# State-space stage of a two-layer kernel: gate copy, score taking and residual adding placed one or two states later, and eight constant products ahead of the first row of C

## The reference, cut to what matters

```python
xz = x @ W_in.T;  xs, z = split(xz)
xc = silu(causal_conv4(xs) + conv_b)
dt, Bm, Cm = split(xc @ W_x.T, [64, 80])
dt = softplus(dt @ W_dt.T + b_dt);  A = -exp(A_log)
h[l, d, n] = exp(dt[l, d] * A[d, n]) * h[l-1, d, n] + dt[l, d] * Bm[l, n] * xc[l, d]
y = sum_n h[l, d, n] * Cm[l, n] + D_param * xc
x = x + ga * ((y * silu(z)) @ W_out.T)
```

## Time and profile before

| | us |
|---|---|
| median of 3 runs | 663.12 (655.6 to 663.97) |
| the profiled execution: its device time | 653.8 |
| the profiled execution: its span in the profile | 651.7 |
| ahead of the state-space loop on VectorE | 32 |
| state-space loop on VectorE | 32 to 278 |
| experts of layer 0, from the first transposed rows to the last row written | 302 to about 403 |
| layer 1 up to its experts, and they | about 403 to 651 |

### The profile page before, as it was taken

How to read it: one execution, slowest core, us unless ns; L and a number is a source line. 1 busy time by engine, 2 the same in 40 slices (tenths; PEclk the granted TensorE clock), 3 DMA queues, 4 the chain that set the end, 5 groups by cost and what they waited for, 6 DMA issues and landing times.

```text
span 651.7 us, 9201 instructions
## 1 busy us (share of the span) xinstructions
PE 511.0 (78%) x2287; PEld 314.1 (48%) x2287; DVE 454.8 (70%) x870; ACT 335.0 (51%) x667; POOL 426.0 (65%) x324
## 2 busy tenths in 40 slices
PE   8879969979997898977998882659887787847420
PEld 4324323423443333455998871225655676746320
DVE  5877989898989799874445531836780686668717
ACT  3757734674677354342333331563741787737605
POOL 2376989898899879703777775510107778777540
PEclk9779979997998968997999996998887899869675
DMA  6423335433223333012655553500026655452025
GB/s 200 129 77 122 134 129 172 138 102 115 97 97 108 115 89 112 13 41 85 184 182 169 159 139 97 197 2 0 17 76 189 209 165 162 131 134 87 32 86 140
DMA packets 47798, 75.47 MB, mean 116 GB/s; under 512 B 6434, under 2 KB 23716, under 8 KB 47620
## 3 DMA queue, kind: packets, MB, share of 16 engines
q1 hardware_dynamic: 42180, 63.48, 31.2%
q0 software_dynamic: 5568, 11.41, 6.7%
HBM read 65.76 MB, written 9.11 MB: 115 GB/s over the span
## 4 chain that ended last, share of the span: by engine, by line
PE 45%; DVE 18%; issue 10%; ACT 9%; POOL 7%; DMA 6%; DVEq 5%; SPq 1%; POOLq 0%
PE ps L1201 14%; PE ps L1164 4%; PE ps L1195 4%; DVE hs L1863 4%; DVEq L1929 4%; POOL y_dram L487 3%; PE ps L1509 3%; PE ps L1537 3%; PE ps L1400 3%; POOL xl L481 3%; DMA y_dram<-ys,rows_i 2%; PE ps L1108 2%; DVE freq L2070 1%; ACT ps L723 1%; DVE prod L1873 1%
## 5 line engine op out<-in xcount | busy, mean ns | idle before, releaser
L533 POOL TENSOR_TENSOR bu<-uT,b_sb 128x1024 f32<-128x1024 f32 x62 | 145.9, 2374 | 2.1 <-DMA b_sb<-b_rows 2.1
L1201 PE MATMUL ps<-prod,cst 128*128 128x512 f32 x256 | 130.2, 653 | 3.2 <-DVE yT L1883 3.2
L481 POOL DMA_INDIRECT xl<-h_dram,rows_i x87 | 87.6, 1007 | 62.0 <-DVE rows_i L1742 36.1
L487 POOL DMA_INDIRECT y_dram<-ys,rows_i x87 | 94.7, 1088 | 33.7 <-issue 23.5
L723 ACT ACTIVATE ps<-dtT,neg_a 128x512 f32<-128x512 f32 x128 | 85.2, 684 | 53.9 <-DVE hs L1863 53.5
L544 POOL TENSOR_TENSOR prod<-hs,c_sb 128x1024 f32<-128x1024 f32 x32 | 76.6, 2393 | 23.5 <-PE ps L1201 14.8
L1201 PEld LDWEIGHTS ps<-prod,cst 128*128 128x128 f32 x256 | 50.1, 206 | 82.8 <-issue 78.0
L1863 DVE TENSOR_TENSOR_SCAN hs<-ps,carry,bu 128x512 f32<-128x512 f32 x64 | 77.5, 1261 | 4.5 <-ACT ps L723 4.5
L1863 DVE TENSOR_TENSOR_SCAN hs<-ps,bu 128x512 f32<-128x512 f32 x64 | 73.9, 1203 | 7.3 <-ACT ps L723 7.1
L1509 PE MATMUL ps<-xt,mfr 128*128 128x128 f32 x384 | 56.3, 303 | 25.3 <-DVE freq L2062 15.9
L1509 PEld LDWEIGHTS ps<-xt,mfr 128*128 128x128 f32 x384 | 52.2, 215 | 28.1 <-issue 27.1
(11 more groups left out here) (289 smaller groups left out, 834.5 us busy)
## 6 DMA issues: line engine op xcount, KB each, us to landing
b_sb<-b_rows SPq DMA_DIRECT2D x31, 512.0 KB
mfr<-in_mf SPq DMA_DIRECT2D x48, 256.0 KB, 3.4
w1r<-in_w SPq DMA_DIRECT2D x39, 256.0 KB
c_sb<-b_rows SPq DMA_DIRECT2D x32, 256.0 KB, 3.5
w_s<-in_w SPq DMA_DIRECT2D x9, 256.0 KB, 3.9
h_dram<-h_tok SPq DMA_DIRECT2D x8, 256.0 KB
down_s<-in_down SPq DMA_DIRECT2D x1, 2048.0 KB, 9.9
xl<-h_dram,rows_i POOLq DMA_INDIRECT x87, 3.6
```

What stands on the lines that cost most here:

```text
L481: pool.indirect_dma_start(xl[:, j % slots, :], None, h_dram[l], bass.IndirectOffsetOnAxis(ap=rows_i[:, 0, j:j + 1], axis=0)).then_inc(load ...
L487: pool.indirect_dma_start(y_dram[l], bass.IndirectOffsetOnAxis(ap=rows_i[:, 1, j:j + 1], axis=0), ys[:, j % XR, :], None).then_inc(saved[j ...
L533: nc.gpsimd.tensor_tensor(bu[:, g % RING, :, :], uT[:, c % 2, :, :], b_sb[:, k % BRING, g % 2, :].unsqueeze(1).broadcast_to([P, ND, CHUNK] ...
L1201: last = nc.tensor.matmul(bank(Y_BANK + d), ident, prod[:, g % RING, d, :], start=n == 0, stop=n == NS - 1)
```

## The change

Four placements in the state-space loop are moved, and one group of products is added. The mathematics and the number of all other instructions stay.

1. ACT: `z_copy(c, 1)` stood at state 15 of the chunk before; it now stands at state 0 of chunk c itself, behind the decays of the next step.
2. ACT and DVE: `add_x` goes from state 6 to 7, `inverse_std` from 9 to 10, and with them on ACT `rstd(1, c)` from 8 to 9.
3. DVE: `take_logits` goes from state 1 to state 3, so from ahead of `gate_y` to behind it (chunks 2 and 3).
4. PE: between the last transposes and the first row of C, a wait for `dt_ready` 1 and `spin(FRONT, 8)`.

```diff
-                      11: lambda c: dt_logs(c, 1), 13: lambda c: z_copy(c, 0), 15: lambda c: z_copy(c, 1)}
-            after = {8: lambda c: rstd(1, c), 12: normed_rows, 14: columns_out}
+                      11: lambda c: dt_logs(c, 1), 13: lambda c: z_copy(c, 0)}
+            after = {9: lambda c: rstd(1, c), 12: normed_rows, 14: columns_out}
...
+                if n == 0 and c:
+                    z_copy(c, 1)
                 if n in before and c + 1 < NCHUNK:
                     before[n](c + 1)
...
             transposes(3)
+            pe.wait_ge(S["dt_ready"], 1)
+            spin(FRONT, 8)
             pe.wait_ge(S["hT_sb"], 4)
...
-            after = {2: gate_y, 6: add_x, 9: inverse_std, 15: router_rows}
+            after = {2: gate_y, 7: add_x, 10: inverse_std, 15: router_rows}
...
-                if n == 1 and c >= 2:
+                if n == 3 and c >= 2:
                     take_logits(0, c - 2, c - 1, E0, BACK, ws0)
```

## The result

The changed kernel took 663.18 us (median of 20 runs, 657.35 to 667.44), the kernel before 658.99 us (20 runs on the same chip, 652.86 to 676.49). The ratio is 1.0094, with a 95% interval of 1.0063 to 1.0124: some 6 us slower, where 4.5 us faster was forecast. The ratio is formed without executions that took over 1.5% more than the fastest of their kernel, so it isn't the ratio of the two medians (1.0064). It is less than the 2% named in the prediction, but its interval excludes both no change and the forecast.

The account below looks back on a forecast made before the run. PE was taken to set the pace in the first halves of chunks 1 and 2, DVE and POOL nearly gapless in second halves. Terms -1.7 + 0.2 + 0.5 - 3.5 = -4.5 us took 663.12 to 658.6; range 648.5 to 666.

Parts of the forecast that it names:

- the 2% named in the prediction: Whole kernel: the difference, 13 us, that a measurement can tell from no change; chance of staying within it 0.92.
- the same two ACT and one DVE operations in another place: 0: State-space loop: moving the square root and inverse_std one state later costs nothing, 0 us.
- The rival of the port: Chunks 1 to 3: inverse_std meets a starting POOL instruction each time, +5.3 us on the forecast, 663.9 us; chance 0.06.
- The rival of the residual: Chunks 1 to 3: the addition adds 1.9 us before state 8's scans in each; +4.1 us in all, 667.2; chance 0.12.
- the 663.12 from which it was worked out: The median time in us of the kernel before, from which the forecast of 658.6 us was taken.
- the forecast's -3.5 us: Chunk 3: the lead kept from the moves, limited by POOL's idle time of 3.5 us; between 0 and -4.1.
- +0.7 us in chunks 1 and 2: Residual addition one state later: DVE waits for state 7's decays, then adds; +0.2 us in chunk 1, +0.5 in chunk 2.
- The +0.2 and +0.5: Later residual addition: loss in us in chunk 1 and chunk 2, where state 9's scans start at 189.0 instead of 188.58.
- forecast at -1.7 us: Ahead of the loop: eight products raise PE's clock earlier, so two halves of z take 2.0 us instead of 3.75.
- its first factor: Ahead of the first row of C: eight products at 0.45 us take 3.6 us, ending where the fourth input's wait ends.
- the 35.6 named as a sign of being wrong: Ahead of the loop: the row of C starting after 35.6 us would show the prediction wrong.

Follow-up runs that it names:

- the control: The kernel before, with only inverse_std written as four tensor_scalar operations on 128x1, each reading one SBUF tensor: 658.74 us, ratio 1.0001.
- the changed kernel with one-tensor operations: All four moves, with inverse_std as four tensor_scalar operations on 128x1, each reading one SBUF tensor; against the kernel before: 658.44 us, ratio 1.0009.
- the probe: The kernel before, inverse_std as four operations reading one SBUF tensor, plus 33 small useless DVE operations in chunks 1 to 3: 673.12 us, ratio 1.0229.

## Why the prediction was wrong

*The step that failed* is "the same two ACT and one DVE operations in another place: 0". It was +5.6 us (1.0094 against 1.0009), some 3 us either way by the two intervals. I had read both prices of the row, 1.06 and 0.17 us, and took them as its bounds; it has no such bound. The rival of the port had the mechanism, but I took it as three meetings of one POOL instruction each and gave it 0.06. It was one meeting, over three POOL instructions (5.16 us; 0.15 and 0.13 in chunks 1 and 2), and its echo in PE's clock was almost as large as itself. It came out at +0.8 us on the kernel before, since the forecast's gains were left in. The rival of the residual came nearest in size (+4.1 against some +6) and had not the mechanism. The absolute times hide the error: 663.18 lies within the range given, but the 663.12 from which it was worked out was high for its kernel, of which 20 runs have a median of 658.99.

*The moves of scores and gate copy* were right in mechanism. In chunk 3 PE does not wait for the gate, its four sums took 1.98 us (3.78 before), and POOL's two waits are gone. Of the forecast's -3.5 us, -2.4 were measured (0.9963), if the stall is kept off; its interval reaches from -5.5 to +0.7. In the traces the stretch of chunk 3 came out 4.3 us shorter than before and 3.1 shorter than in the control, around the forecast. Chunks 1 and 2 gained 0, as said. What the forecast left out is the price of the scores' own second operation at its new place, 0.8 to 1.2 us.

*The residual* was forecast at +0.7 us in chunks 1 and 2 and measured at 0 there (125.13 against 125.36 us between the gates). The +0.2 and +0.5 did stand at state 9 in the changed kernel (estimates from the halves of its rows of four scans: 127.1 us against 126.86, and 189.0 against 188.58). One state on they were gone (130.53 against 130.77, 192.31 against 192.49), since `inverse_std`, 0.49 and 0.62 us before, no longer stood there and took 0.15 and 0.13 behind state 10. Alone and with one-tensor operations it gives +2.2 us (1.0034), of which the interval leaves 0 open. The rival that puts 1.9 us of the residual on the path in each of three chunks did not happen: chunks 1 and 2 show nothing of it.

*The products* were forecast at -1.7 us, the 3.75 us of the halves of z against 2.0 at 2.4 GHz. Between the fourth input and the convolution they brought 0.5 us in the changed kernel, 1.05 alone and 2.7 in the changed kernel with one-tensor operations, where the halves of z took 1.99; the ratio (0.9997) does not resolve that. Where the term failed, it was at its first factor: eight by 0.45 us fill the wait, as in the third of these traces, while 1.89 us left PE standing for 4.5 us, and the clock fell in that wait or just behind it. The forecast took the clock of one execution there for that of the kernel. The row of C began at 35.96, past the 35.6 named as a sign of being wrong; without the products it began later still (36.97), so nothing shows that they hold it back.

*The sum, by the runs*: scores and gate -2.4, residual +2.2, products -0.2 make -0.4 us; all four together with the one-tensor form measured +0.6 (1.0009). That agrees, but each of these numbers has an interval some 4 to 6 us wide. The port adds 5.6.

*What stays open.* What lets one operation on 128x4 in at the next POOL boundary (1.06 us before, 1.77 with the residual alone, 2.32 at most in the probe) and keeps another out over three (8.21 and 8.23 us, 4 times out of 4 at that place). Four operations on one element each were let in one per boundary, and in the row of 8.21 POOL passed three boundaries and then stopped. The Trainium skill ("SBUF — State Buffer", "Who interferes with whom") gives the shared pair to whoever issues first, for the whole instruction. The probe and the four single elements agree, with 2.4 us at most for a POOL instruction of 2.34; the rows of 5.16 and 8.21 do not, and there the measurement decides. Also open is why the part behind the loop took 21.3 us in some executions and 22.9 to 26.0 in others, at a granted clock of 0.50 to 1.00 there.

*The same kind of stall stands elsewhere in the loop.* `dt_and_u` makes u as a product of two SBUF tensors (128x512, 0.69 us where it ran free). In chunk 0, in the kernel before and in its one-tensor control, which don't differ up to there:

```profile
75.44 2.79 DVE L1827 TENSOR_TENSOR uT<-dtT,xcT 128x512 f32<-128x512 f32 x1
78.08 9.68 DVE L1829 TENSOR_TENSOR uT<-dtT,xcT 128x512 f32<-128x512 f32 x1
```

And the POOL instruction at the first boundary inside each:

```profile
77.65 2.80 POOL L544 TENSOR_TENSOR prod<-hs,c_sb 128x1024 f32<-128x1024 f32 x1
80.28 2.33 POOL L544 TENSOR_TENSOR prod<-hs,c_sb 128x1024 f32<-128x1024 f32 x1
```

Where DVE got in at the boundary, POOL's next instruction was 0.45 us longer. Where it did not, it stood until POOL had nothing left to start (87.20). The row took 9.66 to 9.70 us in five of the seventeen traces and 2.75 to 2.79 in twelve. One of the five is that of the changed kernel with one-tensor operations: its stretch of chunk 3 is 57.92 us, 4.6 less than before, and its times show no such gain. So the same list of instructions gives either, and a stall read from one execution need not be in the next. How much of the spread between executions this makes is not shown, and nobody tried another form of this operation.

## What to carry to other kernels

A tiny DVE operation that reads two tensors in SBUF is not cheap beside a POOL that works without a gap: here it cost up to the rest of POOL's run, then POOL waited for DVE, and PE lost its clock. Read its price in the trace wherever POOL is dense, take the longest meeting rather than the mean, and write it as operations on 128x1 that read one tensor, or with one input in PSUM (0.55 and 0.63 us for four here); 128x1 with two tensors took 7.7 us. Before moving anything on DVE, list such operations behind the move: the move shifts their meeting with POOL, and the worth of the move then hangs on them.

No version was shown faster than the kernel before. The best had a ratio of 0.9963 (0.9917 to 1.001), and it is 1.3% faster than the changed kernel by the two ratios.

## What the runs showed of the hardware that I had not expected

- One DVE operation of 0.16 us stood 8.21 to 8.23 us beside POOL, over three boundaries between POOL's instructions, in four kernels.
- Four such operations of one element per partition took 0.8 us and then three times 2.4 us in a row, each from one POOL boundary to the next.
- The same product of two 128x512 tensors, in the same list of instructions, took 2.79 us in one execution and 9.68 in another.
- An operation on one 128x4 tensor and a number per partition took 0.6 to 2.4 us beside POOL; four on 128x1 took 0.55.
- A wait of 4.48 us on PE was followed by a granted clock of 0.50 and 3.8 us of extra time for the next ten products. Before, behind a wait of 0.36 us at the same place, it was 1.00.
